# One layer with attention and a mixture of experts on one core: the experts' first layer takes high and low tokens side by side under the high part of w1, VectorE adds the halves, and POOL makes the low parts of w2

## The chip, the cores and the metric

The kernel runs on 1 core of one Trainium2 chip. Its time is the device time of one execution in microseconds (us), given as the median of several. A core has TensorE (PE, with its weight loads as PEld), VectorE (DVE), ScalarE (ACT), GpSimd (POOL) and SyncE (SP), which here issues all DMA. Each engine works through its own list of instructions in order, and they meet at semaphores.

## The reference

The layer normalises x (8 sequences of 64 tokens, 512 wide), adds cross attention over a context of 1601 tokens, adds an unscaled self attention, and ends with a mixture of experts, which is what the change touches:

```
logits = xf @ gate_w + gate_b                    # xf: 512 tokens x 512, 8 experts
top_v, top_i = jax.lax.top_k(logits, TOP_K)      # TOP_K = 2
cw = cw.at[jnp.arange(T)[:, None], top_i].add(softmax(top_v))
for e in range(8):
    h = jax.nn.relu(xf @ w1[e] + b1[e])          # 512 x 2048
    y = h @ w2[e] + b2[e]                        # 512 x 512
    out = out + cw[:, e:e + 1] * y
```

## The kernel before

**High and low parts.** Every float32 operand of a large product is split in two float32r numbers, a rounded high part and the rest (low part). A product is then three matmul passes, high x high, high x low and low x high (`PASSES`), summed in PSUM. For a weight, ACT copies the raw tile into the high part and another engine subtracts it from the raw tile, which gives the low part: both inputs of that subtraction and its result lie in SBUF.

**The experts.** An expert takes at most 192 tokens (`SLOTS`). Its hidden width of 2048 is cut in 4 pieces of 512 (`NP`), and each piece in 4 blocks of 128 (`FC`, index f). n counts experts, p pieces. Each engine runs expert 0, a hardware loop over experts 1 to 6, and expert 7. On PE one expert is, in order:

- p = 0: `hidden(n, 1)`, `second(n, 0)`, `scatter(n - 1)`
- p = 1: `hidden(n, 2)`, `second(n, 1)`
- p = 2: `gather(n + 1)`, `places(n)`, `hidden(n, 3)`, `second(n, 2)`
- p = 3: `hidden(n + 1, 0)`, `second(n, 3)`

`hidden` is the first layer of one piece: 4 blocks f, each 4 (input chunks c) x 3 passes = 12 matmuls of 192 columns, 48 in all, into two PSUM banks that hold two blocks each. `second` is the second layer of the piece, 20 matmuls of 512 columns into `yb[0]` and `yb[1]`. `gather` picks the expert's tokens (32 matmuls of 192 columns), `places` broadcasts one row, `scatter` returns the outputs in 4 tiles of 4 matmuls (512 columns), where the third tile waits until `add_outputs` on DVE has emptied the first one's bank.

**The chain behind `hidden`.** ACT adds the bias and applies relu into `hf` (L683), POOL copies `hf` into the high part of `h` (L472, L473), DVE subtracts for the low part (L1341, L1343). The next `second` but one reads it, so this chain has a whole `second` of time.

**The weights.** Raw pieces of w1 and w2 (1 MB each) come by DMA into two slots each. For each, ACT makes the high part (`w1_part`, `w2_part`, both through line L487) and DVE the low one (L1209 for w1, L1215 for w2). On both engines this stands ahead of the piece's relu and splits.

Of the kernel before, what the change touches and what calls it, by code (L numbers as in the profile page):

```python
# [39 lines left out]
HB = FC // 2  # L40
# [4 lines left out]
LANES = (slice(0, P), slice(P, 2 * P), slice(2 * P, 2 * P + TAIL), slice(2 * P + TAIL, 3 * P))  # L45
# [115 lines left out]
def layer(nc, x, ctxT, mask, qwT, kwT, vwT, wqT, bias3, v_b, gate_w, gate_b, w1, b1, w2, b2, out):  # L161
    with ExitStack() as top:
# [44 lines left out]
        with ExitStack() as m:  # L207
# [44 lines left out]
            hs = sb(m, "h", [P, 2, FC, 3 * P], F32R)  # L252
            xg = [sb(m, f"xg_{n}", [P, C, SLOTS], F32R) for n in ("hi", "lo")]
# [51 lines left out]
        h_full, h_relu, h_hi, h_lo = sem("hidden_full"), sem("hidden_relu"), sem("hidden_hi"), sem("hidden_lo")  # L305
# [24 lines left out]
        def _(sp):  # L330
# [61 lines left out]
            def expert(ph, e, fresh=False, last=False):  # L392
                for p in range(NP):
                    if p < NP - 1:
                        load_w1(ph, e, p + 1, fresh and p == 0)
                    elif not last:
                        load_w1(ph, e + 1, 0)
                    load_w2(ph, e, p, fresh and p < 2)

            def experts(ph):  # L400
                load_w1(ph, 0, 0, ph == 0)
# [13 lines left out]
        def _(pool):  # L415
# [69 lines left out]
        def _(act):  # L485
# [109 lines left out]
            def w1_part(ph, e, p, fresh=False):  # L595
                s, n = p % 2, e + E * ph
                act.wait_ge(ld_w1[s], 16 * (2 * n + p // 2 + 1))
                if not fresh:
                    act.wait_ge(h_full, HB * (NP * n + p - 1))
# [52 lines left out]
            def gathered(n):  # L652

                for i in range(2):
                    act.wait_ge(xg_full, 2 * n + i + 1)
                    copy(xg[0][:, 2 * i:2 * i + 2], work[2 + i][:, 0:2 * SLOTS].rearrange("p (c n) -> p c n", c=2), xg_hi)
# [9 lines left out]
            def expert(ph, e, fresh=False, first=False, last=False):  # L666
                n = e + E * ph
                for p in range(NP):
                    if p == NP - 1 and not last:
                        w1_part(ph, e + 1, 0)  # L670
                    if p < NP - 1 and not (fresh and p == 0):
                        w1_part(ph, e, p + 1)
                    if not (fresh and p < 2):
                        w2_part(ph, e, p)
                    for f in range(FC):
                        c = FC * (NP * n + p) + f
                        if f % 2 == 0:
                            act.wait_ge(h_full, HB * (NP * n + p) + f // 2 + 1)
                        if not (fresh and p == 0):
                            act.wait_ge(h_lo, c - 3)  # L680
                        col = 16 * e + FC * p + f
                        bias = b1T[:, col:col + 1] if isinstance(e, int) else b1T[:, bass.ds(col, 1)]
                        act.activation(hf[:, f], work[f // 2][:, (f % 2) * SLOTS:(f % 2 + 1) * SLOTS],  # L683
                                       ACT.Relu, bias=bias).then_inc(h_relu, 1)
                    if p == 0 and not first:
                        outputs(n - 1)
                if not last:
                    gathered(n + 1)

            def experts(ph):  # L690
                if ph:
                    w1_part(ph, 0, 0)
                gathered(E * ph)
# [13 lines left out]
        def _(pe):  # L707
# [237 lines left out]
            def hidden(n, p, fresh=False):  # L945
# [62 lines left out]
            def experts(ph):  # L1008
                gather(E * ph)
                hidden(E * ph, 0, ph == 0)  # L1010
                if ph == 0:
                    turn_rows()
# [421 lines left out]
```

## Time and profile before

| | |
|---|---|
| median of 3 executions | 1433.07 us (1432.71 to 1433.19) |
| the profiled execution | 1430.12 us, its span 1428.4 us |
| mean granted TensorE clock | 0.972 of 2.4 GHz |
| busy: PE, PEld | 1343.9 us (94%), 1250.1 us (88%) |
| busy: DVE, ACT, POOL | 854.5 us (60%), 649.4 us (45%), 248.1 us (17%) |
| DMA | 110.36 MB, mean 77 GB/s |

The span reaches from the first to the last instruction. A matmul's record is longer than the distance to the next one's start, since matmuls overlap; the chain of work counts the distances. The experts take the part from about 1020 us to the end.

### The profile page before, as it was taken

The page shows a single profiled execution, that of the slowest core. Times are in us where ns is not written, and L with a number is a line of the kernel's source. Part 1 is how long each engine was busy: PE and PEld are TensorE (multiplying, and loading weights), DVE is VectorE, ACT ScalarE, POOL GpSimd, SP SyncE. Part 2 cuts the span into 40 slices and gives each one's busy share as a digit, 9 for nine tenths or more (in the row PEclk, how much of TensorE's full clock was granted, in tenths as well). Part 3 has the DMA queues.
Part 4 walks back from the last instruction along what each step waited for, and adds up shares of the span by engine and source line. Part 5 has one row for each costly group of instructions (what it writes and reads, how often), then busy time and mean ns, then how long its engine had stood idle before and what let it go on. Part 6 is the DMA issues. An engine that isn't in the chain of part 4 may idle for free.

```text
span 1428.4 us, 26441 instructions
## 1 busy us (share of the span) xinstructions
PE 1343.9 (94%) x9296; PEld 1250.1 (88%) x9296; DVE 854.5 (60%) x2116; ACT 649.4 (45%) x1070; POOL 248.1 (17%) x312
## 2 busy tenths in 40 slices
PE   6999899899989989989989999987799999999996
PEld 6699899899989989989989999976788998899895
DVE  5365556656656565655665656557457676767673
ACT  5245345535534544544553454353335544553441
POOL 3004003101300400400210130010113332333231
PEclk9999999999999999999999999987799999999999
DMA  8001201200200120120120020041135554555440
GB/s 284 1 1 49 74 0 44 78 2 2 86 36 1 49 73 1 49 74 0 35 86 2 1 72 2 1 158 60 60 119 184 188 193 142 178 184 196 147 148 32
DMA packets 57210, 110.36 MB, mean 77 GB/s; under 512 B 2533, under 2 KB 20081, under 8 KB 57081
## 3 DMA queue, kind: packets, MB, share of 16 engines
q1 hardware_dynamic: 57080, 108.66, 22.4%
q8 instruction: 79, 1.29, 0.4%
q14 instruction: 51, 0.41, 0.1%
HBM read 107.60 MB, written 1.05 MB: 76 GB/s over the span
## 4 chain that ended last, share of the span: by engine, by line
PE 89%; DVE 4%; issue 3%; ACT 2%; POOL 1%; DMA 0%; DVEq 0%; SPq 0%; ACTq 0%; POOLq 0%
PE work L714 29%; PE ptp L714 22%; PE ptp L970 10%; PE pv L817 6%; PE work L752 6%; PE ptp L804 6%; PE work L921 2%; PE work L721 1%; PE ptp L941 1%; PE pv L941 1%; DVE summed L1150 1%; PE ptp L721 1%; DVE qT L1157 1%; DVE pt L1141 1%; ACT pt L487 1%
## 5 line engine op out<-in xcount | busy, mean ns | idle before, releaser
L714 PE MATMUL ptp<-vw_hi,cx_hi 128*128 128x256 f32 x832 | 245.6, 295 | 0.0
L430 POOL TENSOR_TENSOR cx_lo<-raw,cx_hi 128x1664 fp32r<-128x1664 f32 x31 | 117.7, 3797 | 719.9 <-ACT cx_hi L487 719.9
L714 PE MATMUL ptp<-vw_lo,cx_hi 128*128 128x256 f32 x832 | 238.6, 287 | 0.0
L714 PE MATMUL ptp<-vw_hi,cx_lo 128*128 128x256 f32 x832 | 238.1, 286 | 0.0
L714 PE MATMUL work<-cx_hi,kw_hi 128*128 128x402 f32 x512 | 179.3, 350 | 9.8 <-DVE cx_lo L1078 8.1
L714 PEld LDWEIGHTS ptp<-vw_hi,cx_hi 128*128 128x128 f32 x832 | 162.8, 196 | 17.9 <-issue 17.9
L714 PE MATMUL work<-cx_lo,kw_hi 128*128 128x402 f32 x512 | 178.4, 348 | 0.0
L714 PE MATMUL work<-cx_hi,kw_lo 128*128 128x402 f32 x512 | 177.6, 347 | 0.0
L1141 DVE TENSOR_TENSOR pt<-ptp,pt 128x512 fp32r<-128x512 f32 (+1 forms) x224 | 141.5, 649 | 46.8 <-ACT pt L487 45.0
L817 PE MATMUL pv<-pt,vv 128*128 128x256 f32 x832 | 152.6, 306 | 16.0 <-DVE qT L1157 13.2
L714 PEld LDWEIGHTS ptp<-vw_lo,cx_hi 128*128 128x128 f32 x832 | 162.8, 196 | 0.0
L714 PEld LDWEIGHTS ptp<-vw_hi,cx_lo 128*128 128x128 f32 x832 | 162.7, 196 | 0.0
L487 ACT ACTIVATE pt<-ptp 128x512 fp32r<-128x512 f32 (+1 forms) x224 | 125.3, 566 | 66.0 <-PE ptp L804 62.8
L1126 DVE CUSTOM_DVE_ANT_0 pr<-work,negmask 128x402 f32<-128x402 f32 x256 | 134.2, 571 | 23.1 <-issue 19.6
L1087 DVE SCALAR_TENSOR_TENSOR kk_lo<-work,biasT,kk_hi 128x402 fp32r<-128x402 f32 x128 | 78.9, 634 | 115.4 <-ACT kk_hi L500 114.9
L554 ACT ACTIVATE pr<-pr,nmx 128x1608 f32<-128x1608 f32 x64 | 104.8, 1637 | 81.8 <-DVE nmx L1134 81.8
L714 PE MATMUL work<-xg_hi,w_hi 128*128 128x192 f32 x512 | 140.5, 274 | 1.3 <-DVE xg_lo L1293 1.3
L714 PE MATMUL work<-xg_hi,w_lo 128*128 128x192 f32 x512 | 140.3, 274 | 0.0
L714 PE MATMUL work<-xg_lo,w_hi 128*128 128x192 f32 x512 | 140.2, 274 | 0.0
L472 POOL CAST h<-hf 128x128 fp32r<-128x128 f32 x128 | 91.8, 718 | 271.4 <-ACT hf L683 271.4
L817 PEld LDWEIGHTS pv<-pt,vv 128*128 128x128 f32 x832 | 113.3, 192 | 24.2 <-issue 16.5
L1120 DVE TENSOR_TENSOR vv<-ptp,vv 128x256 fp32r<-128x256 f32 (+1 forms) x112 | 45.4, 406 | 147.6 <-ACT vv L487 146.4
(188 smaller groups left out, 2717.4 us busy)
## 6 DMA issues: line engine op xcount, KB each, us to landing
w1raw<-in_w SPq DMA_DIRECT2D x32, 1024.0 KB, 5.1
w2raw<-in_w SPq DMA_DIRECT2D x32, 1024.0 KB, 6.0
raw<-in_ctxT SPq DMA_DIRECT2D x32, 832.0 KB, 5.2
pr<-in_mask SPq DMA_DIRECT2D x8, 800.5 KB, 4.5
kwraw<-in_kwT SPq DMA_DIRECT2D x2, 512.0 KB, 4.6
xin<-in_x SPq DMA_DIRECT2D x1, 1024.0 KB, 9.3
qwraw<-in_qwT SPq DMA_DIRECT2D x1, 1024.0 KB, 8.1
pr<-in_vwT SPq DMA_DIRECT2D x2, 512.0 KB, 8.4
```

The costliest lines, as they stand in the source:

```text
L430: pool.tensor_tensor(cx[1][:, :, sl], raw[:, k % 2], cx[0][:, :, sl].bitcast(F32), ALU.subtract).then_inc(c_lo, 1)
L472: pool.tensor_copy(hs[:, p % 2, f, LANES[0]], hf[:, f, 0:P])
L487: act.activation(dst, src, ACT.Copy).then_inc(signal, 1)
L554: act.activation(row, row, ACT.Exp, bias=nmx[:, r:r + 1], accum_out=total).then_inc(exp_done, 1)
L714: last = pe.matmul(dst, lhs(i, c), rhs(j, c), start=(c == 0 and (i, j) == (0, 0)), stop=(c == n - 1 and (i, j) == (1, 0)))
L752: ins = pe.matmul(work[bank_of(last, both[rt])][:, 0:KC], qbd[i][rows, cc, :], kk[j][rows, cc, k * KC:(k + 1) * KC], start=(i, j) == (0, 0 ...
L804: ins = pe.transpose(ptp[j % PTD][:, (2 * n + rt) * P:(2 * n + rt + 1) * P], pr[:, (2 * g + rt) % 4, (first + n) * P:(first + n + 1) * P], ...
L817: last = pe.matmul(pv[:, rt * 2 * P:(rt + 1) * 2 * P], vv[:, kt, g % 2, rt].rearrange("p a d -> p (a d)"), pt[:, j % PTD, n, rt].rearrange ...
L970: last = pe.matmul(yb[st][:], hs[:, s, f, i * P:(i + 1) * P], w2s[k][:, s, f], start=(p == 0 and f == 0 and (i, k) in ((0, 0), (2, 0))), s ...
L1087: dve.scalar_tensor_tensor(out=kk[1][:, m, sl], in0=work[bank][:, 0:KC], scalar=biasT[:, col:col + 1], in1=kk[0][:, m, sl].bitcast(F32), o ...
L1126: dve.tensor_tensor_reduce(pr[:, a % 4, sl], bank[:, 0:KC], negmask[:, sl], SCALE, LOWEST, ALU.add, ALU.max, smx[:, a, k:k + 1]).then_inc( ...
L1141: dve.tensor_tensor(pt[:, j % PTD, 0:n, :, 1, :], ptp[j % PTD][:, 0:n * 2 * P].rearrange("p (n r d) -> p n r d", n=n, r=2), pt[:, j % PTD, ...
```

## The change

- **First layer.** `xg` holds the high tokens (192) and the low tokens (192) side by side. For each f and c there is one matmul of 384 columns under w1's high part, and one of 192 columns under w1's low part, which adds to the first half. A block f now fills its own bank, f % 2, of two banks.
- **Behind it.** ACT adds the bias to the second half and writes it to `hf` (`low_part`); DVE adds the first half (`summed_up`); ACT applies relu into the high part of `h` (`hidden_hi`); DVE makes the low part (`hidden_lo`). PE may begin block f when the sum of block f - 2 is done (`h_sum`).
- **Weights.** POOL makes w2's low part instead of copying `hf`, except for the first two pieces, which stay on DVE. The parts of w1 are made two pieces ahead, and on ACT and DVE all weight parts now stand behind the piece's own blocks.
- **Order.** `gathered` comes ahead of the weight parts of p = 3; `row` and `picks` move from p = 1 to p = 2; at the start of the experts `turn_rows` and `biases` come ahead of a `hidden`.

The core of the diff, in the order of the file: POOL, ACT, PE (`hidden`), DVE:

```diff
             def expert(ph, e, fresh=False):
                 for p in range(NP):
+                    s = p % 2
                     if not (fresh and p < 2):
-                        own(pool, p2_used, NP * n + p - 1)
-                    for f in range(FC):
-                        own(pool, h_relu, FC * (NP * n + p) + f + 1)
-                        pool.tensor_copy(hs[:, p % 2, f, LANES[0]], hf[:, f, 0:P])
-                        pool.tensor_copy(hs[:, p % 2, f, LANES[2]], hf[:, f, P:SLOTS]).then_inc(h_hi, 1)
+                        own(pool, w2_hi, NP * n + p + 1)
+                        pool.tensor_tensor(w2s[1][:, s], w2raw[:, s], w2s[0][:, s].bitcast(F32),
+                                           ALU.subtract).then_inc(w2_lo, 1)
...
+                def low_part(p, f):
+                    c = FC * (NP * n + p) + f
+                    act.wait_ge(h_full, c + 1)
+                    if not (fresh and p == 0):
+                        act.wait_ge(h_lo, c - 3)
...
+                    act.activation(hf[:, f], work[f % 2][:, SLOTS:2 * SLOTS], ACT.Identity, bias=bias).then_inc(h_part, 1)
+
+                def hidden_hi(p, f):
+                    act.wait_ge(h_sum, FC * (NP * n + p) + f + 1)
+                    if f == 0 and not (fresh and p < 2):
+                        act.wait_ge(p2_used, NP * n + p - 1)
+                    act.activation(hs[:, p % 2, f, HI], hf[:, f], ACT.Relu).then_inc(h_hi, 1)
+
                 for p in range(NP):
+                    for f in range(FC):
+                        low_part(p, f)
+                        if f:
+                            hidden_hi(p, f - 1)
+                    hidden_hi(p, FC - 1)
                     if p == NP - 1 and not last:
-                        w1_part(ph, e + 1, 0)
-                    if p < NP - 1 and not (fresh and p == 0):
-                        w1_part(ph, e, p + 1)
+                        gathered(n + 1)
                     if not (fresh and p < 2):
                         w2_part(ph, e, p)
...
+                    if p + 2 < NP:
+                        w1_part(ph, e, p + 2)
+                    elif not last:
+                        w1_part(ph, e + 1, p + 2 - NP)
                     if p == 0 and not first:
                         outputs(n - 1)
...
                 for f in range(FC):
-                    if f % 2 == 0 and not fresh:
-                        pe.wait_ge(h_relu, FC * (NP * n + p) + f - 2)
-                    last = products(work[f // 2][:, (f % 2) * SLOTS:(f % 2 + 1) * SLOTS],
-                             lambda i, c: w1s[i][:, s, c, f * P:(f + 1) * P],
-                             lambda i, c: xg[i][:, c])
-                    if f % 2:
-                        last.then_inc(h_full, 1)
+                    if not (fresh and f < 2):
+                        pe.wait_ge(h_sum, FC * (NP * n + p) + f - 1)
+                    bank = work[f % 2]
+                    for c in range(C):
+                        pe.matmul(bank[:, 0:2 * SLOTS], w1s[0][:, s, c, f * P:(f + 1) * P],
+                                  xg[:, c].rearrange("p i n -> p (i n)"), start=c == 0, stop=False)
+                        last = pe.matmul(bank[:, 0:SLOTS], w1s[1][:, s, c, f * P:(f + 1) * P], xg[:, c, 0],
+                                         start=False, stop=c == C - 1)
+                    last.then_inc(h_full, 1)
...
+                def summed_up(p, f):
+                    dve.wait_ge(h_part, FC * (NP * n + p) + f + 1)
+                    dve.tensor_tensor(hf[:, f], work[f % 2][:, 0:SLOTS], hf[:, f], ALU.add).then_inc(h_sum, 1)
...
                 for p in range(NP):
+                    for f in range(FC):
+                        summed_up(p, f)
+                        if f:
+                            hidden_lo(p, f - 1)
+                    hidden_lo(p, FC - 1)
                     if p == NP - 1 and not last:
-                        w1_part(n + 1, 0)
-                    if p < NP - 1 and not (fresh and p == 0):
-                        w1_part(n, p + 1)
-                    if not (fresh and p < 2):
-                        w2_part(n, p)
+                        gathered(n + 1)
+                    if p == 2:
+                        row(n, e)
+                        if not last:
+                            picks(n + 1)
+                    if p + 2 < NP:
+                        w1_part(n, p + 2)
+                    elif not last:
+                        w1_part(n + 1, p + 2 - NP)
                     if p == 0 and not first:
                         outputs(n - 1)
...
+                    if p == 1 and not first:
+                        add_outputs(n - 1, e - 1)
                     if p == 2:
                         puts(ph, n)
```

**ACT in the loop over the experts, from the last block of piece 0 to the first of piece 1.** Before, these rows stand there (L683 is bias and relu, `w_hi<-w1raw` and `w_hi<-w2raw` the high parts, `y_hi` the high part of the outputs, and in brackets the semaphores waited for):

```order
L683 ACTIVATE hf<-work,b1T 128x192
L662 ISA [waits w2_piece_used]
L487 ACTIVATE y_hi<-ptp 128x512 [waits output_scattered]
L487 ACTIVATE y_hi<-ptp 128x512
L597 ISA
L599 ISA [waits w1_loaded0]
L487 ACTIVATE w_hi<-w1raw 128x2048 [waits hidden_full]
L487 ACTIVATE w_hi<-w2raw 128x2048 [waits w2_piece_used,w2_loaded1]
L678 REGISTER_ALU
L680 ISA [waits hidden_full]
```

With the change, in the same place (L679 is `low_part`, L685 `hidden_hi`):

```order
L679 ACTIVATE hf<-work,b1T 128x192
L685 ACTIVATE h<-hf 128x192 [waits hidden_summed] x2
L607 ISA
L490 ACTIVATE w_hi<-w2raw 128x2048 [waits w2_piece_used,w2_loaded0]
L600 ISA
L602 ISA [waits w1_loaded0]
L490 ACTIVATE w_hi<-w1raw 128x2048 [waits hidden_full]
L665 ISA [waits w2_piece_used]
L490 ACTIVATE y_hi<-ptp 128x512 [waits output_scattered]
L490 ACTIVATE y_hi<-ptp 128x512
L674 REGISTER_ALU
L676 REGISTER_ALU [waits hidden_full]
```

Both weight parts of a piece now follow its last `hidden_hi`, w2's ahead of w1's, and the outputs come behind them.

**DVE at the same place.** Before (L1343 is the last split of a piece, L1312 the outputs' low part, L1209 and L1215 the weights' low parts):

```order
L1343 TENSOR_TENSOR h<-hf,h 128x64
L1311 ISA
L1312 TENSOR_TENSOR y_lo<-ptp,y_hi 128x512 [waits output_hi]
L1311 REGISTER_ALU
L1312 TENSOR_TENSOR y_lo<-ptp,y_hi 128x512 [waits output_hi]
L1208 REGISTER_ALU
L1209 TENSOR_TENSOR w_lo<-w1raw,w_hi 128x2048 [waits w1_hi]
L1215 TENSOR_TENSOR w_lo<-w2raw,w_hi 128x2048 [waits w2_hi]
L1340 ISA
L1341 TENSOR_TENSOR h<-hf,h 128x128 [waits hidden_hi]
```

With the change (L1354 is `summed_up`, L1359 `hidden_lo`, L1229 w1's low part, L1332 the outputs'):

```order
L1359 SCALAR_TENSOR_TENSOR h<-hf,h 128x64
L1228 REGISTER_ALU
L1229 TENSOR_TENSOR w_lo<-w1raw,w_hi 128x2048 [waits w1_hi]
L1331 ISA
L1332 TENSOR_TENSOR y_lo<-ptp,y_hi 128x512 [waits output_hi]
L1331 REGISTER_ALU
L1332 TENSOR_TENSOR y_lo<-ptp,y_hi 128x512 [waits output_hi]
L1353 ISA
L1354 TENSOR_TENSOR hf<-work,hf 128x192 [waits hidden_low_part]
```

One weight part is gone from DVE, and the other stands, with the outputs, between a piece's last split and the first sum of the next piece.

**POOL in the loop.** With the change it holds only this, four times:

```order
L475 TENSOR_TENSOR w_lo<-w2raw,w_hi 128x2048 [waits w2_hi]
L316 REGISTER_ALU
```

The 32 casts of an expert are gone from it, and 4 subtractions of 2048 columns have come.

## Rows read from the trace of the kernel before

**Rows 1.** Busy time by stretch, 1140 to 1240 us.

```profile
1140.00:1240.00 100.00, 100.00 (x662) 89.83 (x661) 69.65 (x119) 47.12 (x59) 34.30 (x72) 1.00 0.53 179
```

**Rows 2.** Chain that ended last, one expert: start us, us, what.

```profile
1099.95 5.34 PE work L714 x48
1105.29 4.58 PE ptp L970 x20
1109.87 3.55 PE work L921 x32
1113.42 0.42 PE ptp L930
1113.84 5.54 PE work L714 x48
1119.38 4.59 PE ptp L970 x20
...
1143.78 0.94 PE ptp L941 x4
...
1147.81 5.34 PE work L714 x48
```

**Rows 3.** The same chain in the attention: 256 and 402 columns.

```profile
411.17 5.94 PE ptp L714 x48
...
427.29 13.21 PE work L714 x72
```

**Rows 4.** Timeline, last matmul of a `hidden` and ACT behind it.

```profile
1166.96 0.28 PE L714 MATMUL work<-xg_hi,w_lo 128*128 128x192 f32 x1
...
1167.45 0.73 ACT L683 ACTIVATE hf<-work,b1T 128x192 f32<-128x192 f32 x2 [1.93 <-PE work L714]
```

**Rows 5.** Groups of instructions, 900 to 1420 us: busy us, mean ns.

```profile
L1209 DVE TENSOR_TENSOR w_lo<-w1raw,w_hi 128x2048 fp32r<-128x2048 f32 x32 | 73.1, 2284 | 7.5 <-ACT w_hi L487 7.0
L487 ACT ACTIVATE w_hi<-w1raw 128x2048 fp32r<-128x2048 f32 x32 | 61.4, 1919 | 0.0
...
L1341 DVE TENSOR_TENSOR h<-hf,h 128x128 fp32r<-128x128 f32 x128 | 41.6, 325 | 20.3 <-POOL h L473 20.1
...
L1320 DVE SCALAR_TENSOR_TENSOR xs<-ptp,cw,xs 128x512 f32<-128x512 f32 x16 | 12.0, 751 | 13.5 <-PE ptp L941 13.5
...
L1305 DVE TENSOR_SCALAR put<-ptp,slot_id 128x512 fp32r<-128x512 f32 x16 | 11.3, 746 | 39.8 <-PE ptp L930 39.8
L1312 DVE TENSOR_TENSOR y_lo<-ptp,y_hi 128x512 fp32r<-128x512 f32 x16 | 10.3, 686 | 30.0 <-ACT y_hi L487 30.0
...
L1293 DVE TENSOR_TENSOR xg_lo<-work,xg_hi 128x384 fp32r<-128x384 f32 x16 | 8.2, 550 | 2.1 <-ACT xg_hi L487 2.1
...
L487 ACT ACTIVATE xg_hi<-work 128x384 fp32r<-128x384 f32 x16 | 7.1, 496 | 7.5 <-PE work L921 7.5
```

**Rows 6.** Groups of instructions of POOL, whole span.

```profile
L430 POOL TENSOR_TENSOR cx_lo<-raw,cx_hi 128x1664 fp32r<-128x1664 f32 x31 | 117.7, 3797 | 719.9 <-ACT cx_hi L487 719.9
...
L463 POOL TENSOR_TENSOR xn_lo<-hn,xn_hi 128x512 fp32r<-128x512 f32 x4 | 5.0, 1271 | 39.2 <-ACT xn_hi L487 39.2
```

**Rows 7.** Timeline of DVE and POOL, 5 to 32 us.

```profile
5.77 1.23 DVE L1069 TENSOR_TENSOR kw_lo<-kwraw,kw_hi 128x1024 fp32r<-128x1024 f32 x1 [4.81 <-ACT kw_hi L487]
...
26.56 3.77 POOL L430 TENSOR_TENSOR cx_lo<-raw,cx_hi 128x1664 fp32r<-128x1664 f32 x1 [2.49 <-ACT cx_hi L487]
...
27.46 3.94 DVE L1069 TENSOR_TENSOR kw_lo<-kwraw,kw_hi 128x1024 fp32r<-128x1024 f32 x1 [3.74 <-ACT kw_hi L487]
```

**Rows 8.** Chain around PE's wait between two batches of the attention.

```profile
397.63 3.46 issue
401.09 1.62 PE work L752 x11
402.71 7.16 PE ptp L714 x48
```

**Rows 9.** Busy time by stretch behind that wait; the clock is the third number from the end.

```profile
402.03:405.44 3.41, 3.41 (x19) 2.94 (x16) 0.53 (x3) 0.00 (x0) 0.00 (x0) 0.50 0.02 5
```

**Rows 10.** Timeline of PE, a wait late in the attention.

```profile
945.94 2.79 PE L804 MATMUL ptp<-ident,pr 128*128 128x128 f32 x12 [3.13 <-issue]
```

**Rows 11.** Chain that ended last, the start of the experts.

```profile
1028.23 5.57 PE work L714 x48
...
1040.02 2.77 PE ptp L980 x6
...
1044.48 7.63 PE ptp L970 x20
1052.11 5.34 PE work L714 x48
```

More of the change, by code:

```diff
@@ L251, in layer @@
                 pre = sb(m2, "pre", [P, TT, P], F32)
-            hs = sb(m, "h", [P, 2, FC, 3 * P], F32R)
-            xg = [sb(m, f"xg_{n}", [P, C, SLOTS], F32R) for n in ("hi", "lo")]
+            hs = sb(m, "h", [P, 2, FC, 2 * SLOTS], F32R)
+            xg = sb(m, "xg", [P, C, 2, SLOTS], F32R)
             pick = sb(m, "pick", [P, TT, SLOTS], F32R)
@@ L393, in expert @@
                 for p in range(NP):
-                    if p < NP - 1:
-                        load_w1(ph, e, p + 1, fresh and p == 0)
+                    if not (fresh and p < 2):
+                        load_w2(ph, e, p)
+                    if p + 2 < NP:
+                        load_w1(ph, e, p + 2)
                     elif not last:
-                        load_w1(ph, e + 1, 0)
-                    load_w2(ph, e, p, fresh and p < 2)
+                        load_w1(ph, e + 1, p + 2 - NP)
             def experts(ph):
-                load_w1(ph, 0, 0, ph == 0)
+                for p in range(2):
+                    load_w1(ph, 0, p, ph == 0)
+                    if ph == 0:
+                        load_w2(ph, 0, p, True)
                 expert(ph, 0, ph == 0)
@@ L685, in expert @@
                     if p == 0 and not first:
                         outputs(n - 1)
-                if not last:
-                    gathered(n + 1)
             def experts(ph):
@@ L692, in experts @@
                     w1_part(ph, 0, 0)
+                    w1_part(ph, 0, 1)
                 gathered(E * ph)
@@ L968, in second @@
                     pe.wait_ge(h_lo, FC * (NP * n + p) + f + 1)
-                    for st, i, k in ((0, 0, 0), (0, 0, 1), (0, 1, 0), (1, 2, 0), (1, 2, 1)):
-                        last = pe.matmul(yb[st][:], hs[:, s, f, i * P:(i + 1) * P], w2s[k][:, s, f],
-                                         start=(p == 0 and f == 0 and (i, k) in ((0, 0), (2, 0))),
-                                         stop=(p == NP - 1 and f == FC - 1 and (i, k) in ((1, 0), (2, 1))))
+                    main, tail = [hs[:, s, f, 0:P], hs[:, s, f, LO_MAIN]], hs[:, s, f, P:2 * P]
+                    begin, end = p == 0 and f == 0, p == NP - 1 and f == FC - 1
+                    pe.matmul(yb[0][:], main[0], w2s[0][:, s, f], start=begin, stop=False)
+                    pe.matmul(yb[0][:], main[0], w2s[1][:, s, f], start=False, stop=False)
+                    pe.matmul(yb[0][:], main[1], w2s[0][:, s, f], start=False, stop=end)
+                    pe.matmul(yb[1][:], tail, w2s[0][:, s, f], start=begin, stop=False)
+                    last = pe.matmul(yb[1][:], tail, w2s[1][:, s, f], start=False, stop=end)
                 last.then_inc(p2_used, 1)
@@ L993, in expert @@
                 for p in range(NP):
+                    if p == 0 and isinstance(n, int) and n == 0:
+                        biases()
                     if p == 2 and not last:
@@ L1001, in expert @@
                         hidden(n + 1, 0)
-                    if p == 0 and isinstance(n, int) and n == 0:
-                        biases()
                     second(n, p)
@@ L1009, in experts @@
                 gather(E * ph)
-                hidden(E * ph, 0, ph == 0)
                 if ph == 0:
                     turn_rows()
+                hidden(E * ph, 0, ph == 0)
                 expert(E * ph, first=True)
@@ L1348, in expert @@
                         biases()
-                    if p == 1:
-                        if not first:
-                            add_outputs(n - 1, e - 1)
-                        row(n, e)
-                        if not last:
-                            picks(n + 1)
+                    if p == 1 and not first:
+                        add_outputs(n - 1, e - 1)
                     if p == 2:
                         puts(ph, n)
-                if not last:
-                    gathered(n + 1)
             def experts(ph):
@@ L1362, in experts @@
                     w1_part(E * ph, 0)
+                    w1_part(E * ph, 1)
                     picks(E * ph)
                     gathered(E * ph)
-                expert(ph, 0, ph == 0, first=True)
+                expert(ph, 0, first=True)
                 with dve.Fori(1, LASTE) as e:
@@ L1385, in _ @@
             step(dve.tensor_tensor(wts[:, 3], wts[:, 1], wts[:, 2], ALU.mult))
-            gathered(0)
             dve.wait_ge(m_full, filled("total"))
@@ L1395, in _ @@
             dve.tensor_scalar(crowded[:], total[:, 0:1], float(SLOTS), None, ALU.is_gt).then_inc(flag_done, 1)
+            gathered(0)
             dve.wait_ge(m_full, filled("places"))
```

43 lines of the change are left out of this document (18 added, 25 removed).

## The prediction

> **What bounds the kernel now.** I read the busy time by stretch first. Between 1140 and 1240 us PE is busy for all of 100 us at the full clock, DVE for 69.65, ACT for 47.12, POOL for 34.30 [rows 1]. The chain of work that ended last says the same: one expert is matmuls end to end [rows 2]. `hidden` takes 5.34 us (48 matmuls, 0.111 us each; 5.54 once), `second` 4.57 (20 of 512 columns), `gather` 3.55, `places` 0.42, `scatter` from 1143.78 to 1147.81, 4.03. An expert is 4 x 5.34 + 0.2 + 4 x 4.57 + 3.55 + 0.42 + 4.03 = 47.9 us. So whatever shortens PE's work counts in full, as long as nobody makes PE wait. The reader should see two things: the gain is on PE, and no other engine is on the path today.
>
> **The gain on PE.** 256 columns take 5.94 / 48 = 0.124 us, 402 take 13.21 / 72 = 0.183 us [rows 3]; 384 in between is 0.176. The 192-column matmul stays at 0.111 [rows 2]. A pair is 0.287 us where three matmuls took 0.333; 16 pairs make a `hidden` of 4.59, 0.75 less. For 32 pieces that is 24 us, or 3.0 per expert. It is also all that the change can give.
>
> The Trainium skill (TensorE: Matmul & The Clock Gate, Back-to-back issue gap) puts a lone matmul of N columns at N / 2.4 + 2.5 ns, which would be 82 ns for 192 and 162 for 384, a `hidden` of 3.9 us. The rows show 111 ns for 192 columns, so they disagree, and with 3.9 us the gain would be 45 us at most.
>
> **The new chain inside `hidden`.** Block f may start when the sum of f - 2 is done. ACT starts 0.21 us after the last matmul's record (1166.96 + 0.28 to 1167.45), and one activation of 192 columns is 0.37 [rows 4]. The sum on DVE is not in the trace: 128 columns from SBUF take 0.325, 384 from PSUM 0.55 [rows 5]; I take 0.35. With 0.05 for each hand-over that is 1.0 us against 1.15 us of block f - 1, whose last record overlaps the next by 0.17. It just doesn't fit: 0.26 us per `hidden` (0 to 0.5), an estimate, where nothing worse waits.
>
> **Something worse: what stands on ACT and DVE behind each piece.** Take the end of `hidden` of piece p as 0.
> - ACT: `low_part` of the last block 0.21 to 0.58, DVE's sum to 0.95, `hidden_hi` 1.0 to 1.37. Then w2's high part to 3.25 and w1's to 5.1 (1.92 each by their records, 1.87 with their overlap) [rows 5].
> - POOL starts w2's low part at 3.3. Its subtraction of 1664 columns takes 3.80 us, of 512 1.27 [rows 6]: 2.19 ns a column, so 4.64 us for 2048. It ends at 7.95.
> - DVE wants to start w1's low part (2.28 us [rows 5]) at 5.1, with both inputs in SBUF, as POOL's. I looked in the trace for two such instructions that overlap, and it has one long case: a DVE subtraction that takes 1.23 us alone began at 27.46, while POOL's ran from 26.56 to 30.33; it took 3.94 us and ended at 31.40 [rows 7]. It did its work after POOL's. So DVE here finishes at 7.95 + 2.28 - 0.15 = 10.1.
> - The first sum of piece p + 1 stands behind that on DVE: 10.1 to 10.45. PE, which began this `hidden` at 4.57 and did two blocks by 6.9, waits until 10.5, and does the other two (2.3, plus 0.2 for the restart) by 13.0. Without the waits it were 9.2.
>
> The Trainium skill (SBUF — State Buffer, Who interferes with whom) has the rule behind that row: a VectorE instruction with two SBUF inputs and a GpSimd one that reads SBUF exclude each other, whichever began first. The one row agrees. It speaks against this change, since POOL is always first.
>
> The four steps of an expert, end of one `hidden` to the end of the next (before: 9.9, 13.9, 14.1, 9.9):
> - p = 0 to 1: `outputs` also stands ahead of the sum, 2 x 0.686 [rows 5]: 11.45, sum 11.8, end **14.3**.
> - p = 1 to 2: `second` and half of `scatter` to 6.4; its third tile waits for `add_outputs` behind w1's low part, 10.1 + 0.75 [rows 5]: 10.9, two tiles 2.05, then `hidden` 4.85: **17.8**.
> - p = 2 to 3: `gather` covers most; `puts`, 2 x 0.746 less overlap [rows 5], is 10.1 to 11.55, sum 11.9, end **14.4**.
> - p = 3 to 0: `gathered` delays ACT by 2 x 0.496 less overlap [rows 5], 0.9: DVE done at 11.0, end **13.9**.
>
> 60.4 against 47.9: 12.5 us more per expert.
>
> **The sum.** Experts 1 to 6: 6 x 12.5 = 75. Expert 0 has the last two steps, +0.3 and +4.0. Expert 7 the first two, +4.4 and +3.9, its third is 0.5 shorter, and its last w2 low part is ready at 8 where `second` wants it at 4.6: +3.4. The start: `hidden` from 1028.23, then the biases at 1040.02, a `second` of 7.63 at half clock, the next `hidden` at 1052.11 [rows 11]. With the biases ahead of the second `hidden`, one wait of 2.8 us and two shorter `hidden` I get 2 us less (-4 to +2). `turn_rows` ahead of the first `hidden` is hidden by the wait for `xg`. The transfers cost nothing: a raw slot is refilled as soon as its low part is made, and ACT reads it nearly two pieces later. Together 75 + 4.3 + 11.2 - 2 = **+88.5**.
>
> **The clock.** After PE stood still for 3.46 us 48 matmuls behind it took 7.16 instead of 5.94 [rows 3, 8], at a granted clock of 0.50, the 1.2 GHz level, for 3.41 us [rows 9]; matmuls after a wait of 3.13 us were slow too [rows 10], and the `second` at 1044.48 took 7.63 where 4.57 is normal [rows 11]. PE now waits 4.5 to 5 us in three of the four steps, 21 times in all. At the low level the 2.3 us behind each wait become about 3.9, and a `scatter` about 2 more: 1.6, 1.6, 2.0. What lies further on is in a `second`, which has 3.6 us to spare. I take it for 85 in 100: 7 x 5.2 x 0.85 = 31, and 2 at the end. None of it would be 33 less, all of it 5 more.
>
> The sum against the profiled execution (1430.1): 1430.1 + 88.5 + 33 = 1552; the median of the runs lies 3 us above that execution, so **1555 us**.
>
> **The rivals.**
> - **DVE is not held up by POOL** (one row is thin evidence). Then DVE is done at 5.1 + 2.28 = 7.4; the steps end at 11.6, 15.1, 13.4, 11.2, 51.3 in all, +3.4 per expert. No wait reaches 3 us, so the clock stays: 6 x 3.4 + 0.6 (expert 0) + 2.9 + 2.9 (expert 7: steps, and its end) - 2 = +25, **1458**. Chance 0.09.
> - **The clock stays high** through waits of 4.5 us, with the rest as forecast: **1522**. For it: PE's waits don't all meet a drop in the same way. Against: the waits of 3.1 and 3.5 us that I looked at did. Chance 0.08, the low end.
> - **The other side: faster.** If w1's low part were done by 6.3 us after a `hidden`, the sums would never be late, and only the 0.26 stays: 32 x (0.75 - 0.26) = 16 us less, **1417**. That is one mechanism, DVE's list clear in time, and the point is 6.3 us. Against it: ACT alone, by rows 5, is not through before 5.1, and DVE needs 2.28 more. Between, up to about 7 us, the time is as before. Chance 0.04, and 0.02 for no change.
> - **Slower still**: POOL's subtraction runs longer in the loop, or the clock stays low through the `second` as well: above **1585**. Chance 0.05.
>
> **How the numbers follow.** The forecast has 0.72. Its own range is 1530 to 1575. The range for all takes in the clock case and reaches toward the unblocked one without holding it: 1505 to 1585. Left out are 1458 (0.09), faster or same (0.06) and 0.05 above, 0.20 in all. About 0.2% can be told from no change here. Faster 0.04, same 0.02, slower 0.94.
>
> **What would show it.** In the profile after: POOL's w2 subtractions at 4.6 us; DVE's w1 low part with a mean near 4.9 us, not 2.28, beginning while POOL's runs; pairs of 384 and 192 columns 0.287 us apart; the chain of waits with PE `work` behind DVE's sum, some 4 us each, three in an expert counting the scatter's; the low clock in many slices behind 1060 us. An expert of about 64 to 65 us. It is wrong if w1's low part stays at 2.28 us, or if ACT's copies run ahead of the last `hidden_hi`.

## The result, and the profile after

The changed kernel takes **1549.59 us** (median of 4 runs, 1546.2 to 1552.56), the kernel before 1432.89 us beside it (4 runs, 1431.87 to 1433.19). The ratio is 1.0815, 95% interval 1.0796 to 1.0835: 117 us slower. The forecast was 1555 us, range 1505 to 1585. The profiled execution took 1549.17 us, its span is 1547.4 us, the mean granted clock 0.942.

From the page of the changed kernel: busy time, the granted clock in 40 slices, the chain of work that ended last by engine, and three groups of instructions.

```profile
PE 1364.9 (88%) x8784; PEld 1261.4 (82%) x8784; DVE 900.3 (58%) x2214; ACT 692.0 (45%) x1198; POOL 268.5 (17%) x86
...
PEclk9999999999999999999999999879899898988988
...
PE 70%; issue 10%; DVE 9%; ACT 8%; POOL 1%; DMA 0%; DVEq 0%; ACTq 0%; SPq 0%; POOLq 0%
...
L970 PE MATMUL work<-xg,w_hi 128*128 128x384 f32 x512 | 180.8, 412 | 67.4 <-DVE hf L1354 67.0
...
L475 POOL TENSOR_TENSOR w_lo<-w2raw,w_hi 128x2048 fp32r<-128x2048 f32 x30 | 137.6, 4586 | 368.5 <-ACT w_hi L490 368.5
L1229 DVE TENSOR_TENSOR w_lo<-w1raw,w_hi 128x2048 fp32r<-128x2048 f32 x32 | 150.3, 4696 | 81.2 <-ACT w_hi L490 81.2
```

The chain of the kernel before, from its page:

```profile
PE 89%; DVE 4%; issue 3%; ACT 2%; POOL 1%; DMA 0%; DVEq 0%; SPq 0%; ACTq 0%; POOLq 0%
```

No engine is busier than PE, and yet the chain that ended last is only 70% PE, where it was 89%: PE waits, 67 us of it for DVE's sum (L1354). DVE's low part of w1 takes 4.70 us on average where [rows 5] had 2.28. Through the experts, the last third of the slices, the clock drops again and again, where [rows 1] had it full.

The waits between 1060 and 1480 us (us in total, times, longest):

```profile
PEld work L970 <- DVE hf L1354: 67.9, 26, 5.0
PE work L970 <- DVE hf L1354: 62.2, 20, 4.7
...
PEld ptp L956 <- DVE xs L1340: 26.4, 6, 4.6
```

The second line has PE's 20 waits for the sum, three per expert, two of them above 4 us (4.27 and 4.73 in one expert) and one of 0.65; besides, there is one wait of some 4 us per expert in `scatter` for `add_outputs` (L1340). They are the two places that the prediction named.

One expert by stretch: the expert as a whole, a wait in it, and what PE did behind that wait.

```profile
1179.50:1244.30 64.80, 51.17 (x259) 45.26 (x258) 39.10 (x68) 27.70 (x44) 18.35 (x4) 0.89 0.37 129
1203.47:1208.50 5.03, 0.93 (x7) 0.70 (x6) 5.03 (x2) 0.84 (x2) 2.74 (x1) 1.00 0.15 27
1208.68:1212.90 4.22, 4.22 (x18) 4.18 (x19) 1.33 (x6) 1.04 (x3) 0.00 (x0) 0.60 0.95 354
```

PE is idle for 13.6 of 64.8 us, where [rows 1] had it busy throughout. Behind a wait of about 4 us it runs at a granted clock of 0.60 on average, mostly at the 1.2 GHz level.

The same wait, seen on three engines. ACT (L679 `low_part`, L685 `hidden_hi`, L490 the high parts), then POOL, then DVE (L1354 `summed_up`):

```profile
1197.72 0.42 ACT L679 ACTIVATE hf<-work,b1T 128x192 f32<-128x192 f32 x1 [0.41 <-PE work L972]
...
1198.57 0.36 ACT L685 ACTIVATE h<-hf 128x192 fp32r<-128x192 f32 x1 [0.17 <-DVE hf L1354]
1198.84 0.86 ACT L490 ACTIVATE xg<-work 128x384 fp32r<-128x384 f32 x2
1199.58 1.92 ACT L490 ACTIVATE w_hi<-w2raw 128x2048 fp32r<-128x2048 f32 x1
1201.38 1.92 ACT L490 ACTIVATE w_hi<-w1raw 128x2048 fp32r<-128x2048 f32 x1
1203.48 0.42 ACT L679 ACTIVATE hf<-work,b1T 128x192 f32<-128x192 f32 x1 [0.18 <-PE work L972]
```

```profile
1201.64 4.57 POOL L475 TENSOR_TENSOR w_lo<-w2raw,w_hi 128x2048 fp32r<-128x2048 f32 x1 [10.41 <-ACT w_hi L490]
```

```profile
1203.33 5.02 DVE L1229 TENSOR_TENSOR w_lo<-w1raw,w_hi 128x2048 fp32r<-128x2048 f32 x1 [2.97 <-ACT w_hi L490]
1208.28 0.61 DVE L1354 TENSOR_TENSOR hf<-work,hf 128x192 f32<-128x192 f32 x2
```

ACT has given DVE the first two blocks by 1205, and DVE sums them only at 1208.28. In between it stands in the low part of w1. POOL ends at 1206.21; 2.28 us, the duration of DVE's subtraction alone, later is 1208.49, and DVE ended at 1208.35. So it did next to nothing while POOL ran, as in [rows 7], and its work after.

PE by timeline, a `hidden` in which nothing waits: pairs of 384 and 192 columns start 0.28 to 0.29 us apart.

```profile
1182.03 0.36 PE L970 MATMUL work<-xg,w_hi 128*128 128x384 f32 x1
1182.23 0.25 PE L972 MATMUL work<-xg,w_lo 128*128 128x192 f32 x1
1182.32 0.36 PE L970 MATMUL work<-xg,w_hi 128*128 128x384 f32 x1
...
1182.60 0.36 PE L970 MATMUL work<-xg,w_hi 128*128 128x384 f32 x1
```

### The profile page after: what moved, and what is told of

It is laid out like the page before. It is cut to its first block, busy times and chain, and to the rows that moved or that the text cites. A ratio compares the mean times of both kernels' runs of the same rounds, so it can differ in the third digit from the quotient of the medians.

```text
span 1547.4 us, 25346 instructions
## 1 busy us (share of the span) xinstructions
PE 1364.9 (88%) x8784; PEld 1261.4 (82%) x8784; DVE 900.3 (58%) x2214; ACT 692.0 (45%) x1198; POOL 268.5 (17%) x86
## 4 chain that ended last, share of the span: by engine, by line
PE 70%; issue 10%; DVE 9%; ACT 8%; POOL 1%; DMA 0%; DVEq 0%; ACTq 0%; SPq 0%; POOLq 0%
PE ptp L729 20%; PE work L729 16%; PE pv L832 6%; PE work L970 6%; PE work L767 6%; PE ptp L819 5%; ACT w_hi L490 5%; PE work L972 2%; DVE w_lo L1229 2%; PE ptp L956 1%; PE work L736 1%; PE pv L956 1%; DVE hf L1354 1%; DVE summed L1170 1%; DVE qT L1177 1%
## 5 line engine op out<-in xcount | busy, mean ns | idle before, releaser
L970 PE MATMUL work<-xg,w_hi 128*128 128x384 f32 x512 | 180.8, 412 | 67.4 <-DVE hf L1354 67.0
L475 POOL TENSOR_TENSOR w_lo<-w2raw,w_hi 128x2048 fp32r<-128x2048 f32 x30 | 137.6, 4586 | 368.5 <-ACT w_hi L490 368.5
L1229 DVE TENSOR_TENSOR w_lo<-w1raw,w_hi 128x2048 fp32r<-128x2048 f32 x32 | 150.3, 4696 | 81.2 <-ACT w_hi L490 81.2
L970 PEld LDWEIGHTS work<-xg,w_hi 128*128 128x128 f32 x512 | 111.8, 218 | 77.8 <-DVE hf L1354 73.2
L490 ACT ACTIVATE pt<-ptp 128x512 fp32r<-128x512 f32 (+1 forms) x224 | 125.1, 567 | 67.9 <-PE ptp L819 65.0
L679 ACT ACTIVATE hf<-work,b1T 128x192 f32<-128x192 f32 x128 | 54.0, 422 | 218.2 <-PE work L972 214.2
L972 PE MATMUL work<-xg,w_lo 128*128 128x192 f32 x512 | 140.5, 274 | 0.0
```

The costliest lines, as they stand in the source:

```text
L475: pool.tensor_tensor(w2s[1][:, s], w2raw[:, s], w2s[0][:, s].bitcast(F32), ALU.subtract).then_inc(w2_lo, 1)
L490: act.activation(dst, src, ACT.Copy).then_inc(signal, 1)
L970: pe.matmul(bank[:, 0:2 * SLOTS], w1s[0][:, s, c, f * P:(f + 1) * P], xg[:, c].rearrange("p i n -> p (i n)"), start=c == 0, stop=False)
L972: last = pe.matmul(bank[:, 0:SLOTS], w1s[1][:, s, c, f * P:(f + 1) * P], xg[:, c, 0], start=False, stop=c == C - 1)
L1229: dve.tensor_tensor(w1s[1][:, s], w1raw[:, s], w1s[0][:, s].bitcast(F32), ALU.subtract).then_inc(w1_lo, 1)
```

## The experiments

"Forecast" below is the mechanism of the prediction. All edits are to the changed kernel unless said otherwise. A time without a number of runs is one run. The kernel before, run beside them on the same chip, took 1430.4 us for e1_pool_cut, e2_w2_on_dve, e4_sums_first and e5_filler, 1431.0 for e3_act_w1_first, e6_four_banks_dve and e7_four_banks_pool, and 1432.1 for the last three (e8, e9, e10), where its 13 runs lie between 1428.79 and 1436.91.

### POOL's subtraction made short (e1_pool_cut)

```diff
-                        pool.tensor_tensor(w2s[1][:, s], w2raw[:, s], w2s[0][:, s].bitcast(F32),
-                                           ALU.subtract).then_inc(w2_lo, 1)
+                        pool.tensor_tensor(w2s[1][:, s, 0, 0:64], w2raw[:, s, 0, 0:64],
+                                           w2s[0][:, s, 0, 0:64].bitcast(F32), ALU.subtract).then_inc(w2_lo, 1)
```

> The changed kernel, but POOL subtracts only 64 of the 2048 columns of each w2 piece (the rest of w2's low part is left out). Theory A (POOL's long subtraction keeps DVE's w1 subtraction out, and the sums stand behind it): w1's low part falls from 4.7 to about 2.3 us, an expert from 64.8 to about 51.3 us, the time to 1450 to 1470 us, and the low clock goes from the experts. Rival B (the new chain of low part, sum and relu makes PE wait, whatever POOL does): about 1545 us.

Measured: 1446.21 us, 4 below the range that I had given it. DVE by groups, 1030 to 1436 us:

```profile
L1229 DVE TENSOR_TENSOR w_lo<-w1raw,w_hi 128x2048 fp32r<-128x2048 f32 x30 | 68.8, 2292 | 81.2 <-ACT w_hi L490 81.2
```

The same DVE instruction, at the same place of its list, is back at 2.29 us when POOL's beside it is 0.32 us long. 103 us of the 117 go. An expert takes 50.6 us (ACT's last block of p = 2 begins at 1256.59 and 1307.20), where the rival "not held up" had 51.3.

Some loss is left. Between 1060 and 1400 us PE still waits for DVE's sum, since w1's low part still stands ahead of it:

```profile
PE work L970 <- DVE hf L1354: 24.3, 14, 2.0
```

And in two of six experts the low clock came, which makes them 52.1 and 52.2 us long. PE by timeline at such a place, then the stretch behind the wait:

```profile
1186.96 0.69 PE L970 MATMUL work<-xg,w_hi 128*128 128x384 f32 x1 [1.97 <-DVE hf L1354]
```

```profile
1187.00:1190.50 3.50, 3.50 (x13) 3.50 (x14) 1.03 (x5) 0.97 (x3) 0.00 (x0) 0.51 0.76 279
```

I had expected that the low clock goes from the experts. It mostly did, but a wait of 2 us was enough twice.

### w2's low part back on DVE (e2_w2_on_dve)

```diff
                         own(pool, w2_hi, NP * n + p + 1)
-                        pool.tensor_tensor(w2s[1][:, s], w2raw[:, s], w2s[0][:, s].bitcast(F32),
-                                           ALU.subtract).then_inc(w2_lo, 1)
...
+                    if not (fresh and p < 2):
+                        w2_part(n, p)
                     if p + 2 < NP:
```

> The changed kernel, but w2's low part is on DVE again, just ahead of w1's low part, and POOL has nothing to do in the experts. Theory A: DVE's list is free at about 7.8 us after a piece instead of 10.1, an expert takes about 52.6 us, the time is 1460 to 1475 us. Rival C (DVE is simply too full for the new chain, so that giving POOL's work back to it makes it worse): above 1550 us.

Measured: 1468.09 us. DVE does both subtractions, one after the other, ahead of the next sum, and that is 81 us better than giving one to POOL. It is still 38 us above the 1430.4 of the kernel before, though POOL does nothing in the experts: PE waits for the sum behind the two subtractions (25.9 us in 13 waits between 1060 and 1400 us, the longest 2.4), and the granted clock between 1150 and 1400 us is 0.95. How the 38 us split between the two was not measured.

### The sums ahead of w1's low part (e4_sums_first)

```diff
                         summed_up(p, f)
+                        if f == 1:
+                            if p < NP - 1:
+                                if not (first and p == 0):
+                                    w1_part(n, p + 1)
+                            elif not last:
+                                w1_part(n + 1, 0)
...
-                    if p + 2 < NP:
-                        w1_part(n, p + 2)
-                    elif not last:
-                        w1_part(n + 1, p + 2 - NP)
```

> The changed kernel, but on DVE w1's low part stands behind the first two sums of the next piece instead of ahead of them; POOL keeps w2's low part and DVE still has to wait for it. Theory A (the place in DVE's list is what makes PE wait): the subtraction still takes 4.5 us and more, but PE waits only about 1 us here and there, an expert takes 46 to 49 us, the time is 1420 to 1445 us. Rival D (the time that POOL and DVE exclude each other is itself the bound, wherever the instruction stands): 1500 us or more.

Measured: 1437.72 us. DVE by groups, 1030 to 1436 us, and by timeline:

```profile
L1229 DVE TENSOR_TENSOR w_lo<-w1raw,w_hi 128x2048 fp32r<-128x2048 f32 x30 | 84.4, 2813 | 0.0
```

```profile
1171.15 4.05 DVE L1229 TENSOR_TENSOR w_lo<-w1raw,w_hi 128x2048 fp32r<-128x2048 f32 x1
...
1182.66 2.80 DVE L1229 TENSOR_TENSOR w_lo<-w1raw,w_hi 128x2048 fp32r<-128x2048 f32 x1
...
1196.88 2.28 DVE L1229 TENSOR_TENSOR w_lo<-w1raw,w_hi 128x2048 fp32r<-128x2048 f32 x1
```

The time came out inside the expectation, its reason only half. I had taken it that the subtraction would still be held up and would merely stand where nobody waits. It also came later, often when POOL was through, and took 2.81 us on average (2.28 to 4.05 in the lines shown). PE's waits for the sum are longer than the 1 us that I had said, up to 2.3, and an expert takes 48.5 us in some and 50.1 in others, not 46 to 49.

### PE kept busy where it waits (e5_filler)

Matmuls whose result nobody reads stand where PE waits, 16 ahead of the third tile of `scatter`, 18 and 22 ahead of the third block of a `hidden`.

```diff
                 for t in range(TT):
+                    if t == 2:
+                        for _ in range(16):
+                            pe.matmul(work[2][:], put[:, 0, 0:P], ys[0][:, 0], start=True, stop=True)
...
                 for f in range(FC):
+                    if f == 2 and p < 2 and not fresh:
+                        for _ in range((18, 22)[p]):
+                            pe.matmul(work[2][:, 0:2 * SLOTS], w1s[0][:, s, 0, 0:P],
+                                      xg[:, 0].rearrange("p i n -> p (i n)"), start=True, stop=True)
```

> The changed kernel with matmuls that nobody reads in a free bank, put where PE waits: 18 and 22 of 384 columns ahead of the third block of the first two hidden pieces, 16 of 512 columns ahead of the scatter's third tile. They are shorter than the waits. Theory A with its clock term of about 31 us: the granted clock stays high in the experts and the time falls to 1512 to 1530 us though PE has more to do. Rival E (the low clock only lies where PE waits anyway, and costs nothing): 1549 us or a little more.

Measured: 1518.30 us, 31.3 less than the changed kernel. By stretch, 1150 to 1400 us, first the changed kernel, then this one:

```profile
1150.00:1400.00 250.00, 198.63 (x1004) 175.04 (x1002) 150.83 (x256) 108.18 (x170) 72.94 (x16) 0.90 0.36 126
```

```profile
1150.00:1400.00 250.00, 236.13 (x1310) 209.34 (x1309) 163.71 (x283) 116.12 (x185) 75.81 (x18) 1.00 0.42 143
```

PE has more to do and the kernel is faster: the granted clock is 1.00 in place of 0.90. The waits themselves are still there (DVE's w1 low part takes 4.88 us). So the loss splits in two here: 31 us of clock, and 86 us that are the waiting less the gain.

### ACT's two copies swapped (e3_act_w1_first, e9_act_w1_first_timed)

```diff
                         gathered(n + 1)
-                    if not (fresh and p < 2):
-                        w2_part(ph, e, p)
                     if p + 2 < NP:
...
                         w1_part(ph, e + 1, p + 2 - NP)
+                    if not (fresh and p < 2):
+                        w2_part(ph, e, p)
```

> The changed kernel with one swap on ACT: behind a piece, w1's high part ahead of w2's. DVE's w1 subtraction is then ready before POOL's w2 subtraction can start. Theory A (whichever of the two begins first keeps the other out): w1's low part falls to 2.3 us, now POOL's subtraction is the one that takes longer than 4.6 us or starts late, and what waits in its place is DVE's low parts of the hidden values, which have two inputs in SBUF too, and PE for w2's low part; an expert takes 50 to 53 us, the time is 1445 to 1475 us. Rival F (POOL always wins): w1's low part stays near 4.7 us and the time near 1550.

Measured: 1433.23 us, below the 1445 to 1475 us that I had given it. DVE and POOL by groups, 1030 to 1425 us, then the timeline of DVE, then of POOL:

```profile
L1359 DVE SCALAR_TENSOR_TENSOR h<-hf,h 128x128 fp32r<-128x128 f32 (+1 forms) x256 | 86.4, 378 | 3.1
L1229 DVE TENSOR_TENSOR w_lo<-w1raw,w_hi 128x2048 fp32r<-128x2048 f32 x30 | 68.8, 2292 | 30.7 <-ACT w_hi L490 30.2
```

```profile
L475 POOL TENSOR_TENSOR w_lo<-w2raw,w_hi 128x2048 fp32r<-128x2048 f32 x30 | 144.5, 4816 | 245.8 <-ACT w_hi L490 245.8
```

```profile
1216.23 2.29 DVE L1229 TENSOR_TENSOR w_lo<-w1raw,w_hi 128x2048 fp32r<-128x2048 f32 x1 [1.16 <-ACT w_hi L490]
1218.63 0.36 DVE L1354 TENSOR_TENSOR hf<-work,hf 128x192 f32<-128x192 f32 x1
1219.77 0.36 DVE L1354 TENSOR_TENSOR hf<-work,hf 128x192 f32<-128x192 f32 x1 [0.78 <-ACT hf L679]
1220.05 3.19 DVE L1359 SCALAR_TENSOR_TENSOR h<-hf,h 128x128 fp32r<-128x128 f32 x2
```

```profile
1218.14 4.81 POOL L475 TENSOR_TENSOR w_lo<-w2raw,w_hi 128x2048 fp32r<-128x2048 f32 x1 [9.44 <-ACT w_hi L490]
```

Now DVE has w1's high part first, starts first and takes its 2.29 us; POOL's record is 0.23 us longer than before: it begins at 1218.14, while DVE still runs (to 1218.52). The sums (L1354), which read one operand from PSUM, pass beside POOL at 0.36 us. What is held up is the split behind them (`hidden_lo`, L1359, both inputs in SBUF): 3.19 us for two. Such holds cost little, since by the order on PE a whole `second` lies ahead of the reader of `h`. An expert takes 48.1 us (ACT's last block of p = 2 begins at 1198.90 and 1247.03). The gain of 2.4 to 3 us per expert goes into a wait of `second` for w2's low part, which now comes last: from 1060 to 1400 us

```profile
PE ptp L988 <- POOL w_lo L475: 13.7, 14, 1.6
```

or 2 us per expert. The expectation for the timed run of the same kernel:

> The changed kernel with the swap on ACT (w1's high part ahead of w2's) once more, timed. Theory: 1433 us as in the first look, within 0.5% of the kernel before: the swap alone takes back all that the change cost, and no more.

Measured: 1432.66 us (10 runs, 1431.09 to 1434.41) beside 1432.1 (13 runs, 1428.79 to 1436.91), ratio 1.0007, interval 0.9997 to 1.0016. The same as the kernel before, with the order of two copies on ACT exchanged.

### Four banks, POOL idle (e6_four_banks_dve)

Block f has its own bank `work[f]`, so PE waits for the sum of one piece earlier; `gather` goes to two of the banks of `yb`, `places` one piece earlier, the low part of w2 to DVE, ahead of that of w1. On DVE `outputs`, `add_outputs` and `row` now also stand ahead of w1's low part, which comes last.

```diff
-                    if not (fresh and f < 2):
-                        pe.wait_ge(h_sum, FC * (NP * n + p) + f - 1)
-                    bank = work[f % 2]
+                    if not fresh:
+                        pe.wait_ge(h_sum, FC * (NP * n + p) + f - 3)
+                    bank = work[f]
...
                     if p == 2:
-                        row(n, e)
+                        puts(ph, n)
                         if not last:
                             picks(n + 1)
+                    if not (fresh and p < 2):
+                        w2_part(n, p)
+                    if p == 0 and not first:
+                        outputs(n - 1)
...
+                    if p == 1:
+                        if not first:
+                            add_outputs(n - 1, e - 1)
+                        row(n, e)
                     if p + 2 < NP:
                         w1_part(n, p + 2)
```

> A version meant to keep the shorter first layer and lose the waits: the first layer writes four banks instead of two, so that PE needs the sum of the same block one piece earlier and not that of two blocks earlier; the next expert's tokens are gathered in the two banks of the scatter, for which the row broadcast moves one piece ahead; w2's low part is on DVE, ahead of w1's, and POOL has nothing to do in the experts. Theory A: DVE has 40 us of work in an expert of 44.9, and a piece's chain of 8 to 9.3 us on it fits the 9.2 us of PE; nothing makes PE wait for long: 1407 to 1420 us. Rival C (DVE too full): 1430 us or more.

Measured: **1411.16 us** (4 runs, 1408.14 to 1412.51), ratio to the kernel before 0.9848, interval 0.9828 to 0.9868. It beats both kernels, the one before by 1.5%. The layer's new form is not what is slow: it needs its sums out of the way of the weights' parts.

### The same with three passes (e8_four_banks_three_passes)

The edit to e6: the matmul of 384 columns cut in two of 192.

```diff
                     for c in range(C):
-                        pe.matmul(bank[:, 0:2 * SLOTS], w1s[0][:, s, c, f * P:(f + 1) * P],
-                                  xg[:, c].rearrange("p i n -> p (i n)"), start=c == 0, stop=False)
+                        pe.matmul(bank[:, SLOTS:2 * SLOTS], w1s[0][:, s, c, f * P:(f + 1) * P],
+                                  xg[:, c, 1], start=c == 0, stop=c == C - 1)
+                    for c in range(C):
+                        pe.matmul(bank[:, 0:SLOTS], w1s[0][:, s, c, f * P:(f + 1) * P], xg[:, c, 0],
+                                  start=c == 0, stop=False)
```

> The four-bank version with w2 on DVE, but the matmul of 384 columns cut in two of 192 (the low tokens' four first), so that PE again issues 48 matmuls of 192 columns for each first-layer piece and all else stays. Theory A (the gain of the change is 0.75 us for each of 32 pieces, all of it on the path): 24 us more than the four-bank version, 1433 to 1437 us, as the kernel before. Rival H (the page's spacing of 82 and 162 ns, a gain of 1.4 us a piece): 1450 us or more. If DVE and not PE bounds the four-bank version: under 1425 us.

Measured: 1431.29 us, 20.1 more than e6 and 2 below the range that I had given it. By stretch, 1150 to 1250 us, first e6, then this one:

```profile
1150.00:1250.00 100.00, 97.86 (x578) 88.11 (x577) 78.10 (x150) 56.69 (x92) 0.00 (x0) 1.00 0.53 183
```

```profile
1150.00:1250.00 100.00, 99.98 (x677) 90.19 (x676) 76.76 (x151) 56.96 (x95) 0.00 (x0) 1.00 0.51 170
```

20 us is what the wide matmul gives in the end; the term was 24. With three passes PE never waits (99.98 of 100), with the wide one it waits 2.1 us in 100, all of it in `scatter` for `add_outputs`, as e6's waits in that stretch say:

```profile
PE ptp L955 <- DVE xs L1341: 2.1, 2, 1.1
```

The steps within the two profiles say the same with less noise: an expert takes 47.86 us here (ACT's last block of p = 3 begins at 1167.85 and 1215.71) and 45.72 in e6 (1160.02 and 1205.74). That is 2.1 apart, and 3.2 with the wait, where the term had 3.0. The wait of 1.1 us an expert is more than the missing 4 us, and is where I put them, but no run takes that wait away, and 4 us lie within what the runs of the kernel before differ by.

### Four banks with POOL (e7_four_banks_pool, e10_four_banks_pool_picks)

The edit to e6: POOL makes w2's low part again, and on DVE w1's low part stands ahead of `outputs`, `add_outputs` and `row` again.

> The same four banks and moved row broadcast, but the weights as in the changed kernel: POOL makes w2's low part, ACT makes w2's high part first. Theory A (besides the two banks, the work behind a piece is a chain through ACT, POOL, DVE and back of about 1.9 + 4.6 + 2.1 + 3.5 = 12 us, longer than PE's 9.2): 1450 to 1480 us. Rival G (only the two banks made PE wait): 1407 to 1420 us, as the other four-bank version.

Measured: 1526.11 us, a clear miss. DVE by timeline, then POOL:

```profile
1179.33 1.40 DVE L1328 TENSOR_SCALAR put<-ptp,slot_id 128x512 fp32r<-128x512 f32 x2
1180.65 5.29 DVE L1309 TENSOR_SCALAR pick<-iota_s,place 128x192 fp32r<-128x192 f32 x4
```

```profile
1180.90 4.69 POOL L475 TENSOR_TENSOR w_lo<-w2raw,w_hi 128x2048 fp32r<-128x2048 f32 x1 [14.28 <-ACT w_hi L490]
```

Four `picks` take 0.99 us where POOL is idle (at 1185.45 in the changed kernel) and 5.29 here. I had put `puts` ahead of them, so that they began with POOL's subtraction, and `gather` waits for them. The mend is to do the picks first:

```diff
                     if p == 2:
-                        puts(ph, n)
                         if not last:
                             picks(n + 1)
+                        puts(ph, n)
```

> The four-bank version with POOL, but the picks ahead of the puts again on DVE. In the run before it four picks took 5.3 us instead of 1.0, because they began while POOL's subtraction ran. Theory A with that: the picks run before POOL starts, gather waits no more, some 4 us less for each of 7 experts and less low clock: 1480 to 1500 us. Rival (the picks had other reasons): 1520 us and more.

Measured: 1486.81 us, 39 less, and the mean of a pick is 314 ns. It is still 54.7 us above the kernel before and 75.7 above e6, with DVE's w1 low part at 4.87 us. PE's largest sum of waits between 1060 and 1460 us is

```profile
PE ptp L989 <- DVE y_lo L1335: 30.3, 6, 5.1
```

for the low part of the outputs, which stands behind w1's low part here and ahead of it in e6. So the 75.7 us hold POOL's subtraction and this order together, and no run takes them apart. Two more banks, with the order that goes with them, give 63 of the 117 us back, not the rest.

## Why the prediction was right

Its steps against what was measured. The steps of an expert are taken between the starts of ACT's last block; the column of the filler shows them with the clock at 1.00.

| | predicted | changed kernel | with filler |
|---|---|---|---|
| pair of matmuls | 0.287 us | 0.28 to 0.29 | |
| POOL's subtraction | 4.64 | 4.59 | |
| w1's low part on DVE | 4.9 | 4.70 (5.0 in the loop) | 4.88 |
| p = 2 to 3, without clock | 14.4 | 14.25 | 14.2 |
| p = 3 to 0 | 13.9, 15.5 with clock | 15.2 | 13.7 |
| p = 0 to 1 | 14.3, 15.9 | 16.1 | 14.1 |
| p = 1 to 2 | 17.8, 19.8 | 19.2 | 17.6 |
| expert | 60.4, 64.8 (85% of the clock) | 64.7 | 59.6 |

- **Gain on PE.** The 0.287 us per pair held. The Trainium skill's formula for a lone matmul (TensorE: Matmul & The Clock Gate, Back-to-back issue gap) would make a pair 0.244 us, an estimate from the page, and does not describe these matmuls. e8 against e6 measures 20 of the 24 us.
- **The chain inside `hidden`** costs less than the 0.26 us that the prediction gave it, for which its own terms (1.0 us against 1.15) show no sum: where nothing else waits, ACT's four blocks begin at 1179.94 and 1183.47, 3.53 us for three blocks of 1.147, which is 0.1.
- **DVE held up by POOL.** Shown by e1 (POOL's instruction short, DVE's 2.29 us) and by e3 (DVE starts first, 2.29 us). What decides it is that ACT makes w2's high part ahead of w1's, so that POOL is first; e3 changes that alone and takes back all 117 us. The Trainium skill's rule (SBUF — State Buffer, Who interferes with whom) agrees with these runs in both halves: that the two exclude each other, and that the order of issue decides who is held up.
- **The clock.** 5.1 us per expert (64.7 less 59.6) where 5.2 was the whole and 4.4 was taken; the chain was 0.8 shorter than its sum (PE's waits are 4.0 to 4.7 us, not 4.5 to 5). That the two errors cancel is luck. The filler's 31 us stand against 33.
- **The ends.** In the profiled executions the difference is 1549.2 - 1430.1 = 119.1 us against 121.5 predicted. The start gave 3 us in place of 2: the last `hidden` of the start ends 0.2 ahead of ACT's L679, so at 1054.3, where [rows 11] give 1052.11 + 5.34 = 1057.4. From the chain of the changed kernel:

```profile
1042.49 0.28 DVE hf L1354
...
1054.54 0.43 ACT hf L679
...
1519.40 4.54 POOL w_lo L475
1523.98 0.79 PE ptp L988
1524.78 0.43 PE ptp L989
```

The last `second` starts at 1523.98, after POOL's w2 low part, and at half clock (0.43 us a matmul, not 0.23), as its term had it. It is ready at 1523.94, 7.9 us after the end of its `hidden` (1516.24 - 0.21), where 8 was predicted. Of the 5.4 us that the forecast is high, 2.4 are these differences; most of the rest is the 3 us that I added for the distance of median and profiled execution, which is 0.4 in the changed kernel.

**The rivals.** "Not held up" (1458) is e1 (1446); its condition failed. Its expert of 51.3 us is nearly e1's (51.1 on average over six); where the other 12 us lie was not followed up. Its step "no wait reaches 3 us, so the clock stays" is not what the runs show. Behind a wait of 1.97 us in e1 the granted clock was 0.51 for 3.5 us, and behind one of 1.94 us in e2 it was 0.54 from 1181.75 to 1185.50, mostly the 1.2 GHz level in both. Behind another wait of 1.94 us in e2, which ends at 1236.68, it was 1.00. In e3, whose waits between 1060 and 1400 us are at most 1.6 us, the clock stayed full from 1066 to 1373 us. "The clock stays high" (1522) is e5 (1518), where a filler had to bring it about. "Faster" (1417) needed w1's low part by 6.3 us after a `hidden`. In e3 it is done at 1218.52, and the `hidden` ended at about 1212.2, which is 6.3 us: just at the point, and the sums are not late. What I had not priced is that w2's low part is then late, and the time is the old one.

## What to carry to other kernels

- Before giving POOL a long elementwise instruction, list what DVE must do beside it and who waits for that. Here two subtractions with all operands in SBUF ran one after the other, so POOL saved DVE 2.3 us per piece and held it up for 2.7. The order in which their inputs are made decides which of them is held up.
- A sum that frees a PSUM bank belongs on DVE's list ahead of work with time to spare, or it needs a bank for each block; count the wait that replaces the saved matmuls, and add the low clock behind it, here a quarter of the loss. Even waits of 2 us can bring it (e1, e2).

## What the runs showed of the hardware

- POOL holds up one-input instructions of DVE too: a pick (TENSOR_SCALAR, SBUF to SBUF, 192 columns) took 4.6 us in e7 in place of 0.31. This agrees with the Trainium skill (SBUF — State Buffer, Who interferes with whom), which names tensor_scalar among the operations that can contend with GpSimd when their operands meet certain conditions.
- The sum, with one operand in PSUM, was not held up beside POOL: 0.36 us at 1218.63 and 1219.77 in e3, both inside POOL's 4.81.
- It works in the other direction as well: POOL's subtraction is 4.82 us on average in e3, where DVE is first and the two records overlap by 0.38 us (at 1218.14), and 4.59 when it is first itself.
